# Sort stage of a graph network kernel: keys, places and ranks written four times each in place of full-width copies

## The chip, the cores and the metric

The kernel runs on one core of one Trainium2 chip. The metric is the device time of the whole program in microseconds (us), as the median of several executions; less is better. Engines are named as in the profile: PE is TensorE, PEld its weight loads, DVE VectorE, ACT ScalarE, POOL GpSimd, SP the engine that issues most DMAs.

## The reference

A two-block graph network over N = 6250 nodes with 64 features and E = 200000 edges (`src`, `dst`; the edges come sorted by `dst`).

```python
h = jnp.maximum(_layernorm(x, axis=-1), 0.0)
x = x + segment_sum(h[src], dst, 6250)
h = jnp.maximum(_layernorm(x, axis=-1), 0.0)
# three layers, out = x = h, row = src, col = dst
for l in range(3):
    f1 = relu(x[row] @ nb_W[l] + nb_b[l])
    f2 = relu(x[col] @ self_W[l] + self_b[l])
    a = relu(concatenate([f1, f2], axis=1) @ att1_W[l] + att1_b[l])
    mask = clip(sigmoid(a @ att2_W[l] + att2_b[l]) * (ZETA - GAMMA) + GAMMA, 0.0, 1.0)
    d_inv_sqrt = clip((segment_sum(mask, row) + 1e-06) ** (-0.5), 0.0, 10.0)
    x = segment_sum(mask * d_inv_sqrt[row] * d_inv_sqrt[col] * x[col], row)
    out = out + x
```

Everything after the sort works on blocks of 128 nodes, and gathers and scatters are matrix products with one-hot matrices. For this the edges must first be sorted into bins, one for each pair (block of `src`, block of `dst`).

## The kernel before, in words

`gnn` runs its stages one after another: `constants`, `load_inputs`, `sort_edges`, `first_table`, `build_and_sum` (which builds the one-hot matrices), then per layer `node_products`, `masks_and_messages` and a path for edges that found no place in their bin. Each stage ends in a barrier of all engines. The change lies in `sort_edges` alone.

**The work of the sort.** There are NB = 49 blocks of nodes. For each block c of `dst`, called a row here, each of the 128 partitions holds a window of WIN = 36 consecutive edges (6 columns by 6 groups) that may belong to the block. NBP = 52 is 49 rounded up. A row has these steps:

- POOL `fetch_key` writes `local`, the 36 keys relative to block c (the block of `src`, if the edge belongs to c), and `fetch_places` writes `place_w`, the places of the edge in its two blocks (two ends, 36 each).
- ACT `widen_blocks` writes each of the 36 keys 52 times side by side into `block_wide`. DVE `pick_blocks` compares that with the numbers 0 to 51 (`k.number`): `hot`, a one-hot row of 52 per edge. Then five compares give `twin`, which tells for the columns 1 to 5 apart whether two edges of one partition have one key.
- PE `count_sooner` (L432, L436) counts with 36 products into `sooner_ps` how many edges come sooner. ACT `take_prefix` (L494) copies that to `sooner`. DVE `pick_ranks` multiplies it with `hot` (`picked`, L570) and adds halves (`folded`, L575). PE `add_ranks` (L447, L451) sums `folded` and `twin` into `rank_ps`, 36 ranks.
- ACT copies the ranks to `rank_few` (L505) and writes each rank 128 times into `rank_wide` (L506). DVE `spread_out` (L581) compares them with `k.ranks`: `spread`, a one-hot row of 128 per edge.
- DVE `set_values` writes `hot` times the place for each end into `value`. The first end reads `place_wide`, which ACT `widen_places` (L488) has written 52 times each (L564). The second end reads `place_w` itself, with a step of 0 over the 52 elements (L561).
- PE `scatter` (L461) sums `value` times `spread` over the 36 edges into `bins_ps`; ACT `take_bins` copies the bins to bytes, SP stores them, POOL `note_spills` (four dependent steps, L394 to L397) marks edges whose rank has no place.

**The order.** Each engine has its own order of these steps, written by hand; `each_row` unrolls row 0 and loops over the rest two at a time (buffers b = 0 and 1), and counting semaphores tie the engines. `row(c)` is:

```python
# DVE                        # PE                         # ACT
pick_ranks(c, b)             add_ranks(c, b)              rank_few(c); rank_wide(c)
pick_blocks(c + 1, 1 - b)    count_sooner(c + 1, 1 - b)   take_prefix(c + 1, 1 - b)
spread_out(c - 1, 1 - b)     scatter(c - 1, 1 - b)        widen_blocks(c + 2, b)
set_values(c, b)                                          widen_places(c + 1, 1 - b)
                                                          take_bins(c - 1, 1 - b)
```

POOL's `row(c)` is `fetch_key(c + 2)`, `fetch_places(c + 1)`, `note_spills(c - 1)`. So one row's ranks go round a ring: `folded` on DVE, `add_ranks` and then the next row's `count_sooner` on PE, `take_prefix` on ACT, `picked` and `folded` on DVE again. `block_wide` and `place_wide` have one buffer each; `widen_blocks(c)` waits for `hot` of row c - 1, `widen_places(c)` for the values of row c - 1.

Of the kernel before, what the change touches and what calls it, by code (L numbers as in the profile page):

```python
# [14 lines left out]
P = 128  # L15
# [6 lines left out]
WIN = COLS * GROUPS  # L22
BLOCK_KEY = 64
# [315 lines left out]
def sort_edges(nc, k):  # L339
# [6 lines left out]
    with ExitStack() as st:  # L346
# [6 lines left out]
        local = sb("local", [P, 2, WIN], BF16)  # L353
# [4 lines left out]
        block_wide = sb("block_wide", [P, WIN, NBP], BF16)  # L358
        place_wide = sb("place_wide", [P, WIN, NBP], BF16)
        rank_wide = sb("rank_wide", [P, 2, WIN, P], BF16)  # L360
# [13 lines left out]

        with phase(nc, "passed keyed placed blocks_wide places_wide hot_ready twins_ready values_ready prefixed prefix_ready "
# [5 lines left out]
            def _(pool):  # L381
                def fetch_key(c, b):
                    at = bass.ds(pool.value_load(k.starts[0:1, bass.ds(c, 1)]), WIN)
                    pool.tensor_tensor(local[:, b, :], k.key[:, at], k.bases[:, bass.ds(c, 1)].to_broadcast([P, WIN]),
# [90 lines left out]
            def _(act):  # L475
# [3 lines left out]
                def widen_blocks(c, b):  # L479
                    act.wait_ge(s["keyed"], c + 3)  # L480
                    act.wait_ge(s["hot_ready"], c + 2)
                    nc.scalar.activation(block_wide[:, :, :], local[:, b, :].unsqueeze(2).to_broadcast([P, WIN, NBP]),
                                         ACT.Copy).then_inc(s["blocks_wide"], 1)

                def widen_places(c, b):
                    act.wait_ge(s["placed"], c + 3)
                    act.wait_ge(s["values_ready"], c + 2)
                    nc.scalar.activation(place_wide[:, :, :], place_w[:, b, 0, :].unsqueeze(2).to_broadcast([P, WIN, NBP]),  # L488
# [12 lines left out]
                def row(c, b, nth, first):  # L501
# [4 lines left out]
                    nc.scalar.activation(rank_wide[:, b, :, :], rank_ps[b][:, :].unsqueeze(2).to_broadcast([P, WIN, P]),  # L506
# [32 lines left out]
            def _(dve):  # L539
# [3 lines left out]
                def pick_blocks(c, b):  # L543
# [4 lines left out]
                    nc.vector.tensor_tensor(by_column[:, b, :, :], k.number[:, 0:NBP].unsqueeze(1).to_broadcast([P, WIN, NBP]),  # L548
                                            block_wide[:, :, :], ALU.is_equal).then_inc(s["hot_ready"], 1)
                    dve.wait_ge(s["ranked"], c + 1)  # L550
                    for by in range(1, COLS):
                        z = (COLS - by) * GROUPS
                        last = nc.vector.tensor_tensor(twin[:, b, by - 1, 0:z], local[:, b, by * GROUPS:WIN],
                                                       local[:, b, 0:z], ALU.is_equal)
                    last.then_inc(s["twins_ready"], 1)

                def set_values(c, b):
                    dve.wait_ge(s["hot_ready"], c + 3)
                    dve.wait_ge(s["placed"], c + 3)
# [1259 lines left out]
```

## Time and profile before

| | us |
|---|---|
| median of 3 runs | 4062.88 |
| lowest and highest | 4059.52, 4064.14 |
| time of the profiled execution | 4065.69 |
| its span in the trace | 4063.8 |
| mean granted clock of TensorE | 0.965 |

Busy shares over the whole span are PE 92%, DVE 82%, POOL 60%, ACT 56%. The sort runs from about 37 to 511 us of the span; the rows of `sort_edges` lie in its first eighth. In the profile's slices the granted clock stands at 8 or 7 tenths there and at 9 or more behind it. The granted clock is given as a share of full speed: a mean over a stretch, in which the clock stood at 1.0 (2.4 GHz) for a part and at 0.5 (1.2 GHz) for the rest. In a timeline, each line has the start, the duration, the engine, the line of the code, what is written and read, the count, and in brackets how long the engine sat idle before it and what ended that.

### The profile page before, as it was taken

Reading aid. Unit: us, or ns where it says so; the run is one execution under the profiler, and the core shown is the slowest. Engines: PE = TensorE matmul, PEld = TensorE weight load, DVE = VectorE, ACT = ScalarE, POOL = GpSimd, SP = SyncE. Lnnn points to the kernel's source line nnn. Section 1 sums busy time; section 2 is a strip of 40 time slices with the busy share of each in tenths; the row PEclk is TensorE's granted clock in tenths of the full one; section 3 lists DMA queues with packets and bytes.
Section 4 is the critical chain, followed back from the end, with each engine's and each line's share of the span. In section 5 each row is a group of like instructions: output and inputs, shape, how many; then the busy total and the mean of one; then the engine's idle time right before and its main releaser. Section 6 shows DMA issues by size and latency. Waiting matters only on the chain. (4 is left out here: it accounts for less than half of the span.)

```text
span 4063.8 us, 258198 instructions
## 1 busy us (share of the span) xinstructions
PE 3726.6 (92%) x99855; PEld 3570.8 (88%) x99856; DVE 3323.0 (82%) x5561; ACT 2293.6 (56%) x5432; POOL 2420.1 (60%) x4693
## 2 busy tenths in 40 slices
PE   4888758888879999999998999999998999999998
PEld 4777658888859999899997999999997999989998
DVE  7999968888867888788877888878886788878887
ACT  4988858888841111388881111168884111138887
POOL 2667723333325666577774666667775566657776
PEclk8888879999989999999999999999999999999999
DMA  1000169999937777677754777767773777767775
GB/s 36 15 15 14 16 211 333 342 338 335 336 114 234 241 243 249 194 190 190 190 160 162 243 240 248 248 167 190 190 190 111 238 243 248 243 193 191 190 190 154
DMA packets 586269, 800.05 MB, mean 197 GB/s; under 512 B 126790, under 2 KB 528154, under 8 KB 586170
## 3 DMA queue, kind: packets, MB, share of 16 engines
q1 hardware_dynamic: 550106, 719.89, 56.9%
q0 software_dynamic: 36064, 78.85, 6.6%
q8 instruction: 61, 1.00, 0.1%
q14 instruction: 38, 0.31, 0.0%
HBM read 672.34 MB, written 126.04 MB: 196 GB/s over the span
## 5 line engine op out<-in xcount | busy, mean ns | idle before, releaser
L1359 PE MATMUL pre_ps<-rows_a,hot_ab 128*128 128x64 bf16 x21609 | 1296.1, 193 | 48.1 <-ACT rows_a L1452 23.2
L1359 PE MATMUL pre_ps<-table,hot_ab 128*128 128x64 bf16 x21609 | 1294.9, 193 | 1.7 <-issue 1.7
L1359 PEld LDWEIGHTS pre_ps<-rows_a,hot_ab 128*128 128x128 fp8e4 x21609 | 1127.6, 98 | 78.1 <-issue 54.7
L1593 POOL TENSOR_TENSOR message<-message 128x448 f32<-128x448 f32 x1029 | 948.5, 934 | 322.2 <-DVE message L1661 321.7
L1359 PEld LDWEIGHTS pre_ps<-table,hot_ab 128*128 128x128 fp8e4 x21609 | 1129.1, 98 | 0.6 <-issue 0.6
L1643 DVE SCALAR_TENSOR_TENSOR message<-pre_ps,all_w 128x448 f32<-128x448 f32 x1029 | 642.9, 625 | 280.6 <-PE pre_ps L1359 193.2
L1403 PE MATMUL pre_ps<-table,hot_ab 128*128 128x64 bf16 x21609 | 805.7, 194 | 19.8 <-DVE message L1661 9.1
L1403 PEld LDWEIGHTS pre_ps<-table,hot_ab 128*128 128x128 fp8e4 x21609 | 763.9, 98 | 22.8 <-issue 22.1
L1500 ACT ACTIVATE message<-pre_ps 128x448 bf16<-128x448 f32 x1029 | 674.1, 674 | 165.0 <-DVE pre_ps L1655 139.2
L1655 DVE TENSOR_TENSOR pre_ps<-pre_ps,mask 128x448 f32<-128x448 f32 x735 | 465.0, 633 | 209.5 <-PE pre_ps L1403 187.4
L1626 DVE TENSOR_REDUCE logit<-message 128x7 f32<-128x448 f32 x1029 | 626.8, 609 | 0.0
L1661 DVE TENSOR_TENSOR message<-pre_ps,message 128x448 f32<-128x448 f32 x1029 | 620.9, 615 | 2.2 <-ACT message L1500 0.5
L1448 ACT ACTIVATE gate<-logit,all_b 128x49 f32<-128x49 f32 x147 | 49.9, 339 | 720.1 <-DVE logit L1626 720.1
L897 POOL DMA_DIRECT2D places<-slots_scratch x294 | 213.9, 742 | 398.5 <-DVE hot L1014 319.2
L1489 ACT ACTIVATE pre_ps<-pre_ps,mask 128x64 f32<-128x64 f32 x2058 | 442.7, 309 | 0.2
L1415 PE MATMUL pre_ps<-message,hot_ab 128*128 128x192 bf16 x3675 | 402.6, 248 | 2.8 <-POOL message L1593 2.0
L1014 DVE TENSOR_SCALAR hot<-places,pcol 128x1792 uint8<-128x1792 uint8 x343 | 379.8, 1149 | 10.6 <-DMA places<-slots_scratch 10.6
L1415 PE MATMUL total_ps<-message,hot_ab 128*128 128x192 bf16 x3528 | 382.6, 246 | 0.7 <-issue 0.7
L989 ACT ACTIVATE counts<-cnt_ps 128x896 bf16<-128x896 f32 x343 | 314.1, 916 | 1.5 <-PE cnt_ps L951 1.0
L1415 PEld LDWEIGHTS pre_ps<-message,hot_ab 128*128 128x128 fp8e4 x3675 | 293.4, 97 | 5.4 <-issue 4.7
L1465 ACT ACTIVATE table<-left 128x64 f32 (+1 forms) x147 | 37.8, 257 | 444.1 <-POOLq L1570 444.1
L965 PE MATMUL l_ps<-rows,counts 128*128 128x64 bf16 x7203 | 269.6, 194 | 15.2 <-issue 9.9
(195 smaller groups left out, 5526.0 us busy)
## 6 DMA issues: line engine op xcount, KB each, us to landing
hot_ab<-hot_scratch SPq DMA_DIRECT2D x2058, 224.0 KB, 4.0
hot_scratch<-hot SPq DMA_DIRECT2D x343, 336.0 KB, 5.8
both<-hot_scratch SPq DMA_DIRECT2D x147, 784.0 KB, 5.1
places<-slots_scratch POOLq DMA_DIRECT2D x196, 224.0 KB, 6.3
places<-slots_scratch POOLq DMA_DIRECT2D x98, 336.0 KB, 7.3
slots_scratch<-bins SPq DMA_DIRECT2D x392, 16.0 KB, 1.4
out<-res SPq DMA_DIRECT2D x1, 1536.0 KB
raw<-in_src SPq DMA_DIRECT2D x1, 768.0 KB
```

Source lines behind the costliest of these rows:

```text
L989: nc.scalar.activation(counts[:, n.half, :, :], cnt_ps[n.half][:, 0:G, :], ACT.Copy)\
L1014: dve.tensor_scalar(hot[:, n.slot, 0:2, :], places[:, n.h, :, n.g * G * P:(n.g + 1) * G * P], k.pcol1[:, 0:1], float(HOT), ALU.is_equal, A ...
L1359: last = nc.tensor.matmul(pre_ps[g][:, j, :], hot[:, b, g, end, j * P:(j + 1) * P].bitcast(FP8), table, start=end + part == 0, stop=end == ...
L1403: last = nc.tensor.matmul(bank(g, b)[:, j, :], hot[:, 1 - b, g, 0, j * P:(j + 1) * P].bitcast(FP8), k.table_s[:, g * G + j, part, :], star ...
L1415: last = nc.tensor.matmul(sum_ps[b], hot[:, 1 - b, g, 1, j * P:(j + 1) * P].bitcast(FP8), top[:, g, j, :, :, 1], start=t == 0, stop=t == N ...
L1489: last = nc.scalar.activation(bank(g, b)[:, j, :], bank(g, b)[:, j, :], ACT.Copy, scale=k.mask[:, bass.ds(r * NB + g * G + j, 1)])
L1500: nc.scalar.activation(top[:, g, :, 0, :, 1], bank(g, b), ACT.Copy).then_inc(s["tops_ready"], 1)
L1593: pool.tensor_tensor(message[:, g, :, 2, :], message[:, g, :, 1, :], top[:, g, :, 1, :, 1], ALU.subtract).then_inc(s["third_ready"], 1)
L1626: dve.tensor_reduce(logit[:, b, g * G:(g + 1) * G], weighed[(b + g) % 2], X, ALU.add)\
L1643: dve.scalar_tensor_tensor(weighed[(b + g) % 2], pre_ps[g][:, 0:G, :], 0.0, k.w3[:, :].unsqueeze(1).to_broadcast([P, G, D]), ALU.max, ALU. ...
L1655: dve.tensor_tensor(bank(g, b), bank(g, b), k.mask[:, bass.ds(r * NB + g * G, G)].unsqueeze(2).to_broadcast([P, G, D]), ALU.mult).then_inc ...
L1661: dve.tensor_tensor(message[:, g, :, 1, :], bank(g, b), top[:, g, :, 0, :, 1], ALU.subtract).then_inc(s["rest_ready"], 1)
```

## The change

Where before an engine read 52 or 128 full copies of a value, it now reads four copies of it, again and again:

- ACT writes each key (`block_four`), each place of both ends (`place_four`) and each rank (`rank_four`) four times side by side instead of 52 or 128 times. `block_four` and `place_four` have two buffers, and ACT's waits for them are one row older.
- DVE reads them with a pattern of three dimensions: 36 edges, then 13 (or 32) repeats with a step of 0, then 4 elements with a step of 1. Output and the other input are cut into runs of four in the same way.
- Both ends of `set_values` now read `place_four` in this way; the second one read `place_w` with a step of 0 before. DVE no longer waits for `placed` itself.
- One compare of 180 elements takes the place of the five for `twin`. It reads `local` in five overlapping stretches of 36 from element 6, 12, ... 30 on; `local` has 30 more elements for this, set to zero once by a memset ahead of the rows.

Nothing outside `sort_edges` changes; the stage of messages is the same in both kernels.

```diff
-        local = sb("local", [P, 2, WIN], BF16)
+        TURN = WIN - GROUPS
+        local = sb("local", [P, 2, WIN + TURN], BF16)
...
-        block_wide = sb("block_wide", [P, WIN, NBP], BF16)
-        place_wide = sb("place_wide", [P, WIN, NBP], BF16)
-        rank_wide = sb("rank_wide", [P, 2, WIN, P], BF16)
+        block_four = sb("block_four", [P, 2, WIN, FOUR], BF16)
+        place_four = sb("place_four", [P, 2, 2, WIN, FOUR], BF16)
+        rank_four = sb("rank_four", [P, 2, WIN, FOUR], BF16)
...
+        def fours(t):
+            return t.rearrange("p w (m f) -> p w m f", f=FOUR)
+
+        def along(four, m):
+            return four.unsqueeze(2).to_broadcast([P, WIN, m, FOUR])
+
+        def later_columns(b):
+            row = local[:, b, GROUPS:GROUPS + WIN]
+            return bass.AP(row.tensor, row.offset, [row.ap[0], [GROUPS, COLS - 1], [1, WIN]])
...
                 def widen_blocks(c, b):
                     act.wait_ge(s["keyed"], c + 3)
-                    act.wait_ge(s["hot_ready"], c + 2)
-                    nc.scalar.activation(block_wide[:, :, :], local[:, b, :].unsqueeze(2).to_broadcast([P, WIN, NBP]),
+                    act.wait_ge(s["hot_ready"], c + 1)
+                    nc.scalar.activation(block_four[:, b, :, :], local[:, b, 0:WIN].unsqueeze(2).to_broadcast([P, WIN, FOUR]),
                                          ACT.Copy).then_inc(s["blocks_wide"], 1)
 
                 def widen_places(c, b):
                     act.wait_ge(s["placed"], c + 3)
-                    act.wait_ge(s["values_ready"], c + 2)
-                    nc.scalar.activation(place_wide[:, :, :], place_w[:, b, 0, :].unsqueeze(2).to_broadcast([P, WIN, NBP]),
+                    act.wait_ge(s["values_ready"], c + 1)
+                    nc.scalar.activation(place_four[:, b, :, :, :], place_w[:, b, :, :].unsqueeze(3).to_broadcast([P, 2, WIN, FOUR]),
                                          ACT.Copy).then_inc(s["places_wide"], 1)
...
-                    nc.scalar.activation(rank_wide[:, b, :, :], rank_ps[b][:, :].unsqueeze(2).to_broadcast([P, WIN, P]),
+                    nc.scalar.activation(rank_four[:, b, :, :], rank_ps[b][:, :].unsqueeze(2).to_broadcast([P, WIN, FOUR]),
                                          ACT.Copy).then_inc(s["ranks_wide"], 1)
...
-                    nc.vector.tensor_tensor(by_column[:, b, :, :], k.number[:, 0:NBP].unsqueeze(1).to_broadcast([P, WIN, NBP]),
-                                            block_wide[:, :, :], ALU.is_equal).then_inc(s["hot_ready"], 1)
+                    nc.vector.tensor_tensor(fours(by_column[:, b, :, :]),
+                                            fours(k.number[:, 0:NBP].unsqueeze(1).to_broadcast([P, WIN, NBP])),
+                                            along(block_four[:, b, :, :], NBP // FOUR), ALU.is_equal)\
+                        .then_inc(s["hot_ready"], 1)
                     dve.wait_ge(s["ranked"], c + 1)
-                    for by in range(1, COLS):
-                        z = (COLS - by) * GROUPS
-                        last = nc.vector.tensor_tensor(twin[:, b, by - 1, 0:z], local[:, b, by * GROUPS:WIN],
-                                                       local[:, b, 0:z], ALU.is_equal)
-                    last.then_inc(s["twins_ready"], 1)
+                    nc.vector.tensor_tensor(twin[:, b, :, :], later_columns(b),
+                                            local[:, b, 0:WIN].unsqueeze(1).to_broadcast([P, COLS - 1, WIN]), ALU.is_equal)\
+                        .then_inc(s["twins_ready"], 1)
...
                 def set_values(c, b):
                     dve.wait_ge(s["hot_ready"], c + 3)
-                    dve.wait_ge(s["placed"], c + 3)
                     dve.wait_ge(s["scattered"], c + 1)
-                    nc.vector.tensor_tensor(value[:, b, :, HALF:HALF + NBP], by_column[:, b, :, :],
-                                            place_w[:, b, 1, :].unsqueeze(2).to_broadcast([P, WIN, NBP]), ALU.mult)
                     dve.wait_ge(s["places_wide"], c + 3)
-                    nc.vector.tensor_tensor(value[:, b, :, 0:NBP], by_column[:, b, :, :], place_wide[:, :, :], ALU.mult)\
-                        .then_inc(s["values_ready"], 1)
+                    for end in range(2):
+                        last = nc.vector.tensor_tensor(fours(value[:, b, :, end * HALF:end * HALF + NBP]),
+                                                       fours(by_column[:, b, :, :]),
+                                                       along(place_four[:, b, end, :, :], NBP // FOUR), ALU.mult)
+                    last.then_inc(s["values_ready"], 1)
...
-                    nc.vector.tensor_tensor(spread[:, :, :], k.ranks[:, :].unsqueeze(1).to_broadcast([P, WIN, P]),
-                                            rank_wide[:, b, :, :], ALU.is_equal).then_inc(s["spread"], 1)
+                    nc.vector.tensor_tensor(fours(spread[:, :, :]), fours(k.ranks[:, :].unsqueeze(1).to_broadcast([P, WIN, P])),
+                                            along(rank_four[:, b, :, :], P // FOUR), ALU.is_equal).then_inc(s["spread"], 1)
...
                 nc.vector.memset(value[:, :, :, :], 0.0).then_inc(s["step"], 1)
-                dve.wait_ge(s["step"], 1)
+                nc.vector.memset(local[:, :, WIN:WIN + TURN], 0.0).then_inc(s["step"], 1)
+                dve.wait_ge(s["step"], 2)
```

DVE's instructions of one row in the loop before, from `picked` to the second value:

```order
L570 TENSOR_TENSOR picked_w<-hot_w,sooner_w 128x1872
L575 TENSOR_TENSOR folded_w<-picked_w 128x936
L544 REGISTER_ALU
L548 TENSOR_TENSOR hot_w<-number,block_wide 128x1872
L553 TENSOR_TENSOR twin<-local 128x30
L553 TENSOR_TENSOR twin<-local 128x24
L553 TENSOR_TENSOR twin<-local 128x18
L553 TENSOR_TENSOR twin<-local 128x12
L553 TENSOR_TENSOR twin<-local 128x6
L580 REGISTER_ALU
L581 TENSOR_TENSOR spread<-ranks,rank_wide 128x4608
L561 TENSOR_TENSOR value_w<-hot_w,place_w 128x36x52
```

The same row in the changed kernel:

```order
L582 TENSOR_TENSOR picked_w<-hot_w,sooner_w 128x1872
L587 TENSOR_TENSOR folded_w<-picked_w 128x936
L556 REGISTER_ALU
L560 TENSOR_TENSOR hot_w<-number,block_four 128x1872
L565 TENSOR_TENSOR twin<-local 128x180
L592 REGISTER_ALU
L593 TENSOR_TENSOR spread<-ranks,rank_four 128x4608
L574 TENSOR_TENSOR value_w<-hot_w,place_four 128x36x52 x2
```

The order is the same; five compares have become one, and the instructions write as many elements as before, the compare for `twin` apart (180 instead of 90).

## Rows read from the trace of the kernel before

**Rows 1.** Windows: from:to, length; PE, PEld, DVE, ACT, POOL busy; granted clock; DMA.

```profile
100.00:450.00 350.00, 302.49 (x4025) 271.19 (x4023) 346.58 (x431) 313.46 (x235) 251.68 (x231) 0.88 0.10 15
```

**Rows 2.** Timeline: DVE from one row's folded to the next row's folded.

```profile
313.84 0.65 DVE L575 TENSOR_TENSOR folded_w<-picked_w 128x936 bf16<-128x936 bf16 x1
...
314.40 1.17 DVE L548 TENSOR_TENSOR hot_w<-number,block_wide 128x1872 bf16<-128x1872 bf16 x1
...
315.50 0.48 DVE L553 TENSOR_TENSOR twin<-local 128x30 bf16<-128x30 bf16 x5
...
315.90 2.60 DVE L581 TENSOR_TENSOR spread<-ranks,rank_wide 128x4608 bf16<-128x4608 bf16 x1
...
318.43 2.11 DVE L561 TENSOR_TENSOR value_w<-hot_w,place_w 128x1872 bf16<-128x1872 bf16 x1
...
320.46 1.19 DVE L564 TENSOR_TENSOR value_w<-hot_w,place_wide 128x1872 bf16<-128x1872 bf16 x1
...
321.57 1.12 DVE L570 TENSOR_TENSOR picked_w<-hot_w,sooner_w 128x1872 bf16<-128x1872 bf16 x1
...
322.73 0.65 DVE L575 TENSOR_TENSOR folded_w<-picked_w 128x936 bf16<-128x936 bf16 x1
```

**Rows 3.** Timeline: the ring of one early row, at half clock throughout.

```profile
61.34 0.65 DVE L575 TENSOR_TENSOR folded_w<-picked_w 128x936 bf16<-128x936 bf16 x1
...
62.23 1.86 PE L447 MATMUL rank_ps<-folded_w,identb 128*128 128x36 bf16 x26 [2.76 <-DVE folded_w L575]
...
64.06 1.72 PE L432 MATMUL sooner_ps<-hot_w,later 128*128 128x312 bf16 x6
...
65.58 4.00 PE L436 MATMUL sooner_ps<-hot_w,onesb 128*128 128x260 bf16 x30
...
69.69 0.52 ACT L494 ACTIVATE sooner_w<-sooner_ps,rank 128x312 bf16<-128x312 f32 x1 [1.21 <-PE sooner_ps L436]
...
70.24 1.13 DVE L570 TENSOR_TENSOR picked_w<-hot_w,sooner_w 128x1872 bf16<-128x1872 bf16 x1 [1.30 <-ACT sooner_w L494]
...
71.41 0.65 DVE L575 TENSOR_TENSOR folded_w<-picked_w 128x936 bf16<-128x936 bf16 x1
```

**Rows 4.** Timeline: PE in two later rows, one fast, one slowed.

```profile
316.55 0.95 PE L432 MATMUL sooner_ps<-hot_w,later 128*128 128x312 bf16 x6
...
317.34 2.19 PE L436 MATMUL sooner_ps<-hot_w,onesb 128*128 128x260 bf16 x30
...
323.52 1.86 PE L447 MATMUL rank_ps<-folded_w,identb 128*128 128x36 bf16 x26 [1.97 <-DVE folded_w L575]
...
325.35 1.72 PE L432 MATMUL sooner_ps<-hot_w,later 128*128 128x312 bf16 x6
...
326.86 3.10 PE L436 MATMUL sooner_ps<-hot_w,onesb 128*128 128x260 bf16 x30
```

**Rows 5.** Groups of instructions on PE, 100 to 450 us: count, busy us, mean ns, idle before.

```profile
L436 PE MATMUL sooner_ps<-hot_w,onesb 128*128 128x260 bf16 (+4 forms) x1170 | 107.8, 259 | 0.0
...
L447 PE MATMUL rank_ps<-folded_w,identb 128*128 128x36 bf16 x1022 | 73.2, 243 | 47.5 <-DVE folded_w L575 47.5
L432 PE MATMUL sooner_ps<-hot_w,later 128*128 128x312 bf16 x234 | 52.1, 376 | 0.0
```

**Rows 6.** Groups of instructions on ACT, 100 to 450 us.

```profile
L506 ACT ACTIVATE rank_wide<-rank_ps 128x4608 bf16<-128x4608 f32 x39 | 156.3, 4007 | 0.0
...
L505 ACT ACTIVATE rank_few<-rank_ps 128x36 f32<-128x36 f32 x39 | 7.9, 202 | 31.8 <-PE rank_ps L451 31.8
```

**Rows 7.** Groups of instructions on POOL, 100 to 450 us: the two fetches.

```profile
L389 POOL COPY place_w<-place 128x72 bf16 x38 | 41.0, 1078 | 19.8 <-issue 13.5 <-DVE value_w L564 5.6 <-ACT place_wide L488 0.7
L384 POOL TENSOR_TENSOR local<-key,bases 128x36 bf16 x38 | 38.9, 1025 | 50.0 <-DVE value_w L564 21.8 <-issue 20.3 <-DVE twin L553 6.8
```

**Rows 8.** Timeline: a POOL fetch beside DVE's spread.

```profile
486.19 2.54 DVE L581 TENSOR_TENSOR spread<-ranks,rank_wide 128x4608 bf16<-128x4608 bf16 x1
...
487.06 1.78 POOL L384 TENSOR_TENSOR local<-key,bases 128x36 bf16 x1 [1.13 <-DVE twin L553]
```

More of the change, by code:

```diff
@@ L22 @@
 WIN = COLS * GROUPS
+FOUR = 4
 BLOCK_KEY = 64
@@ L383, in fetch_key @@
                     at = bass.ds(pool.value_load(k.starts[0:1, bass.ds(c, 1)]), WIN)
-                    pool.tensor_tensor(local[:, b, :], k.key[:, at], k.bases[:, bass.ds(c, 1)].to_broadcast([P, WIN]),
+                    pool.tensor_tensor(local[:, b, 0:WIN], k.key[:, at], k.bases[:, bass.ds(c, 1)].to_broadcast([P, WIN]),
                                        ALU.subtract).then_inc(s["keyed"], 1)
@@ L594, in _ @@
                 spread_out(NB - 1, 0)
-                centre_rows(k, s, Chain(dve, s["step"], 1))
+                centre_rows(k, s, Chain(dve, s["step"], 2))
 def nodes(k, t):
```

## The prediction

> **What bounds the sort now.** I read the windows first, because the change touches only the sort. Between 100 and 450 us DVE is busy for 346.6 of 350 us, ACT for 313.5, PE for 302.5 and POOL for 251.7 [rows 1]. The groups of PE give the number of rows in that stretch: 1170 products of L436 at 30 a row are 39 rows [rows 5], so a row takes 350 / 39 = 8.97 us. All 49 rows lie in the sort; nothing outside it is changed.
>
> Next the timeline of one row on DVE [rows 2]. From one `folded` (313.84) to the next (322.73) are 8.89 us without a gap. The starts give what each instruction costs the row: `folded` 0.56, `hot` 1.10, the five compares of `twin` 0.40, `spread` 2.53, the second end's values (L561) 2.03, the first end's (L564) 1.11, `picked` 1.16. L561 and L564 write equally many elements; L561 reads its place with a step of 0 and takes nearly twice as long. So **DVE sets the row**, and what it loses in instructions the row loses, down to the next limit.
>
> That limit is the ring. Its parts show best in an early row in which PE ran at the half level of its clock throughout [rows 3]: `folded` to PE's first product 0.89; L447 to L432 1.83; the count itself, from L432's start to L436's end, 69.58 - 64.06 = 5.52; then 0.11 to ACT's `take_prefix`, 0.55 to `picked`, 1.17 to `folded`. The sum is 10.07. Without the count it is 4.55. The same count takes 319.53 - 316.55 = 2.98 at the full level, and in a row that the half level covers in part 329.96 - 325.35 = 4.61 [rows 4]. The ring is thus 7.53 in a fast row, 9.16 in a slowed one. A slowed row hardly shows today, since 9.16 is only just over 8.97. The mean count is 107.8 / 39 + 52.1 / 39 less the 0.16 by which the two groups overlap [rows 4, 5], which is 3.94. With a fast count at 2.98 and a slowed one at about 4.5, some 0.64 of the rows must be slowed. The mean clock of 0.88 [rows 1] says the same: a quarter of the time at the half level.
>
> **The change, part by part.**
>
> *L561 becomes a second L564.* Both ends now read four copies with a step of 1. From 2.03 to 1.11 is 0.92 us a row, if a run of four keeps the rate of a long run. No row of this trace has so short a run. The nearest rows from both sides are L564 (52 elements in a run, 1.11) and L561 (a run of one, 2.03). I take 1.11: L561 differs from L564 by the step of 0 between neighbours, and the new pattern has a step of 1 between three of four. The cost if that is wrong is the third rival.
>
> The Trainium skill has two rules on this. The Vector Engine (DVE) Microarchitecture Reference, "Measured stream behaviour on trn2", has a port at full rate as long as its elements come in runs of at least two adjacent 4-byte words on an 8-byte boundary, with any hop between; four bf16 are exactly that. Against the change speaks SBUF — State Buffer, "The DMA port swizzle": lines have 16 bytes and each access that crosses to a new line pays; runs of four hop to another line twice as often as a full line would need. By the first rule the sum stands as I make it; by the second it would move towards the third rival. No row here tells them apart.
>
> *Five compares become one.* Now 0.40. One instruction of 180 elements: at the slope between L564 and `spread`, (2.53 - 1.11) / (4608 - 1872) = 0.52 ns for an element, 180 of them lie 0.88 under L564's 1.11, at 0.23; counted from `folded` (0.56 for 936) the same slope gives 0.17. I take 0.20, between 0.17 and, if overlapping reads cost what five instructions did, 0.40. Gain 0.20 (0 to 0.23).
>
> *`hot` and `spread`* write as many elements as before at the same rate: nothing, with the same condition on runs of four.
>
> *ACT's copies.* 36 elements take 0.202 and 4608 take 4.007 [rows 6], 0.83 ns for each. `rank_four` (144) is then 0.29, `block_four` about 0.3, `place_four` (288) 0.41. ACT drops from 313 of 350 us to some 2.1 us a row. That gives nothing by itself: ACT's work lies beside DVE's. It only makes `take_prefix` start 0.1 after the count in each row, where before it could stand behind 4.0 us of `rank_wide`; I have reckoned the ring with 0.11. If that cover went the other way, ACT has 5 us a row to spare.
>
> *The memset* of 60 elements comes once, at most 0.2 us, behind the large one that is there. *Waits:* those that go were long fulfilled; POOL still waits for `values_ready` before it fetches places, and ACT's older waits only let it run earlier.
>
> **The sum.** DVE needs 8.89 - 0.92 - 0.20 = 7.77 in the row shown; there `hot` and L564 ran at 1.17 and 1.19, where `picked` takes 1.12 for as many elements [rows 2], so about 7.7. The ring at full clock, 7.53, is just under that. At the half level it now sticks out: a slowed row takes about 4.55 + 4.5 - 0.1 (`folded` to PE is 323.52 - 322.73 = 0.79 in the later row [rows 2, 4]) = 8.95. So the gain hangs on how many rows stay slowed:
>
> - none: 7.7, a gain of 1.27 a row;
> - as many as now (0.64): 0.36 x 7.7 + 0.64 x 8.95 = 8.50, a gain of 0.47;
> - my choice, 0.42 of the rows: 0.58 x 7.7 + 0.42 x 8.95 = 8.2, a gain of 0.77.
>
> The reason for my choice: slow stretches follow stretches in which PE waits and then runs only the small products of L447. That wait is 47.5 / 39 = 1.22 us a row now [rows 5]. A fast row now can wait 1.97 [rows 4]; with 1.2 us less to a row it waits about 0.8, while a slowed row waits no less than today. The mean falls by some four tenths, and I let the share of slowed rows fall by a third.
>
> The gain counts in 46 of the 48 row-to-row steps; the first two, like the row of [rows 3], are set by the ring at half clock and stay. 46 x 0.77 = 35 us. Against the profiled execution's 4065.7 that is 4030.7; the median shown is 2.8 us below that execution, which gives **4028**.
>
> **The rivals.**
>
> 1. *The clock recovers.* PE waits so little that the slow stretches vanish. For: the wait falls, and each slow row shortens the wait before the next. Against: the small products stay and are still 1.8 us of a row. Gain 46 x 1.27 = 58 us: 4004.
> 2. *The clock stays as it is,* in share of rows: 46 x 0.47 = 22: 4041. POOL can lead to nearly the same place. Its steps wait for DVE's instructions: a fetch of 36 elements that started 0.87 after `spread` ended 0.11 after its end, 1.78 us long [rows 8]. Of 350 us it was held by a named semaphore for only 5.6 + 0.7 + 21.8 + 6.8 = 34.9 [rows 7], so it needs (350 - 34.9) / 39 = 8.08 us a row, more than DVE's new 7.7. Against that: its six steps mostly end with one DVE instruction each, and DVE still has seven to a row. If POOL sets a row of 8.6, the gain is 46 x 0.37 = 17: 4046. The Trainium skill, SBUF — State Buffer, "Who interferes with whom", says that a DVE instruction with two SBUF inputs keeps out a GpSimd one that reads SBUF; by that rule, the trace agrees.
> 3. *Slower: runs of four run at L561's rate.* Place: `hot`, `spread` and both values. Price: 0.92 for each of the three of 1872 elements and 0.92 x 4608 / 1872 = 2.26 for `spread`, 5.0 us; a row of 12.7, a loss of 3.8 in 46 rows: 4236. It decides from the point at which a quarter of it is lost: 1.27 / 5.0. For: no such pattern in the trace, and the repeat of 13 is a new dimension. Against: above.
> 4. *Half of it:* hops cost a little, say 0.2 to 0.3 of that loss. DVE's row is then 8.7 to 9.2 and the time 4053 to 4075.
>
> **How the numbers follow.** The forecast has a chance of 0.50, rival 1 of 0.17, rival 2 of 0.20, rival 3 of 0.07, rival 4 of 0.06. About 0.2%, some 8 us, is what a measurement of this kernel can tell from no change. The forecast and rivals 1 and 2 lie beyond that on the fast side, 0.87; rival 4 gives 0.03 to the same and 0.02 to slower, the rest to faster; rival 3 is slower. So faster 0.88, same 0.03, slower 0.09. The range takes in rival 1 with a little over it, since DVE's row could come at 7.6 with the shortest steps (46 x 1.37 = 63), and rival 2 with POOL: 3997 to 4046.
>
> **What would show it.** Right: DVE's two value instructions alike at about 1.15 us, one compare for `twin` near 0.25, `spread` still 2.55; ACT's copies at 0.3 to 0.45; DVE no longer without gaps, with idle time before `picked`, released by ACT's `sooner_w`, in just those rows in which the count takes over 4 us; a mean clock between 100 and 400 us above 0.88. The rest of the program unchanged. Wrong: `hot` or `spread` longer than before (rivals 3 and 4); rows of 7.7 throughout at a clock near 1 (rival 1); ACT or DVE waiting for POOL's `local` or `place_w` (POOL in rival 2).

## The result, and the profile after

| | before | changed kernel |
|---|---|---|
| median | 4062.19 us | 4024.85 us (4022.69 to 4027.73, 4 runs) |
| profiled execution | 4065.69 | 4025.11 |
| its span | 4063.8 | 4023.2 |
| ratio to before | | 0.9909, 95% interval 0.9892 to 0.9926 |

Forecast were 4028 us and a range of 3997 to 4046. The change is faster by 37 us.

The windows of the changed kernel, 100 to 400 us of the span; columns as in [rows 1]:

```profile
100.00:400.00 300.00, 271.93 (x3712) 247.77 (x3709) 277.28 (x254) 61.96 (x216) 212.93 (x215) 0.91 0.11 16
```

DVE was busy for 99% of a stretch and is now for 92%; ACT fell from 90% to 21%; the granted clock went from 0.88 to 0.91. DVE is no longer the only thing that sets a row. Its groups of instructions in the same stretch (count, busy us, mean ns, idle before it and what ended that):

```profile
L593 DVE TENSOR_TENSOR spread<-ranks,rank_four 128x4608 bf16<-128x4608 bf16 x36 | 91.7, 2547 | 0.0
L574 DVE TENSOR_TENSOR value_w<-hot_w,place_four 128x1872 bf16<-128x1872 bf16 x74 | 82.5, 1154 | 0.0
L560 DVE TENSOR_TENSOR hot_w<-number,block_four 128x1872 bf16<-128x1872 bf16 x36 | 41.8, 1162 | 0.0
L582 DVE TENSOR_TENSOR picked_w<-hot_w,sooner_w 128x1872 bf16<-128x1872 bf16 x36 | 41.5, 1152 | 21.5 <-ACT sooner_w L506 21.5
...
L565 DVE TENSOR_TENSOR twin<-local 128x180 bf16<-128x180 bf16 x36 | 10.1, 282 | 0.0
```

Both value instructions take 1.15 us, where L561 took 2.11 [rows 2]. `hot` and `spread` are as fast as with full-width copies (1.17 and 2.60 in [rows 2]). DVE now waits 21.5 us, all of it ahead of `picked`, for `sooner_w`. The waits say how often:

```profile
DVE picked_w L582 <- ACT sooner_w L506: 21.5, 15, 1.5
```

15 times in 36 rows, up to 1.5 us. The timeline shows one such row in full, and a fast one ahead of it:

```profile
303.54 0.65 DVE L587 TENSOR_TENSOR folded_w<-picked_w 128x936 bf16<-128x936 bf16 x1
...
311.22 0.65 DVE L587 TENSOR_TENSOR folded_w<-picked_w 128x936 bf16<-128x936 bf16 x1
...
312.15 1.86 PE L459 MATMUL rank_ps<-folded_w,identb 128*128 128x36 bf16 x26 [0.99 <-DVE folded_w L587]
...
313.98 1.08 PE L444 MATMUL sooner_ps<-hot_w,later 128*128 128x312 bf16 x6
...
314.85 3.76 PE L448 MATMUL sooner_ps<-hot_w,onesb 128*128 128x260 bf16 x30
...
318.72 0.52 ACT L506 ACTIVATE sooner_w<-sooner_ps,rank 128x312 bf16<-128x312 f32 x1 [4.05 <-PE sooner_ps L448]
...
319.28 1.13 DVE L582 TENSOR_TENSOR picked_w<-hot_w,sooner_w 128x1872 bf16<-128x1872 bf16 x1 [1.49 <-ACT sooner_w L506]
...
320.44 0.65 DVE L587 TENSOR_TENSOR folded_w<-picked_w 128x936 bf16<-128x936 bf16 x1
```

From 303.54 to 311.22 are 7.68 us: a row at DVE's pace. From 311.22 to 320.44 are 9.22: `folded` to PE 0.93, L459 to L444 1.83, the count 4.63 instead of 2.98, 0.11, 0.56, 1.16. Over the whole sort the 46 steps behind the first two are of just these two kinds: 26 of 7.54 to 7.74 us, 20 of 9.09 to 9.22, mostly by turns. In all of the 20 the count takes 4.62 to 4.64 us and `picked` waits for it; in all of the 26 it takes 2.98 or 2.99 and `picked` waits for nothing.

**Where the time went.** `folded` came first at 51.47 and last at 484.12 us before, at 51.35 and 453.62 now; that is 30.4 us less over 48 steps. The first product behind the sort's barrier started at 511.33 and now starts at 479.67, 31.7 us earlier, since the last `spread` and its scatter also gained. The span is 40.6 us shorter. The other 8.9 lie behind the sort, in code that the change does not touch; the section on the forecast comes back to this.

### The profile page after: what moved, and what is told of

It reads as the page before. It is cut to its first block and busy times, and to the rows that moved or that the text cites. A ratio compares the mean times of both kernels' runs of the same rounds, so it can differ in the third digit from the quotient of the medians.

```text
span 4023.2 us, 257999 instructions
## 1 busy us (share of the span) xinstructions
PE 3711.7 (92%) x99855; PEld 3565.5 (89%) x99856; DVE 3262.2 (81%) x5362; ACT 1976.7 (49%) x5432; POOL 2380.6 (59%) x4693
## 5 line engine op out<-in xcount | busy, mean ns | idle before, releaser
L1027 DVE TENSOR_SCALAR hot<-places,pcol 128x1792 uint8<-128x1792 uint8 x343 | 379.6, 1148 | 8.7 <-DMA places<-slots_scratch 8.7
L1428 PEld LDWEIGHTS total_ps<-message,hot_ab 128*128 128x128 fp8e4 x3528 | 278.0, 96 | 0.1
```

The source lines that it names most:

```text
L1027: dve.tensor_scalar(hot[:, n.slot, 0:2, :], places[:, n.h, :, n.g * G * P:(n.g + 1) * G * P], k.pcol1[:, 0:1], float(HOT), ALU.is_equal, A ...
L1428: last = nc.tensor.matmul(sum_ps[b], hot[:, 1 - b, g, 1, j * P:(j + 1) * P].bitcast(FP8), top[:, g, j, :, :, 1], start=t == 0, stop=t == N ...
```

## The experiments

Three questions stood open. Which parts of the change were needed? Are the rows of 9.1 us really the clock's? Has POOL a part in it? All kernels below build on the changed kernel unless it is said otherwise. To read them I use, beside the time, what a trace tells exactly: the mean of the 46 row steps, the granted clock between 100 and 400 us, and the start of the first product behind the sort (its end).

| kernel | mean row | shortest, longest | clock | sort's end | ratio to before |
|---|---|---|---|---|---|
| before | 8.97 | 8.85, 9.29 | 0.88 | 511.3 | 1 |
| changed | 8.32 | 7.54, 9.22 | 0.91 | 479.7 | 0.9909 (0.9892 to 0.9926) |
| x1, second end with step 0 | 8.87 | 8.59, 9.22 | 0.89 | 505.0 | 0.9979 (0.9969 to 0.9988) |
| x2, ranks 128 times | 8.88 | 8.59, 9.23 | 0.88 | 507.4 | 0.9980 (0.9971 to 0.9990) |
| x3, two products added | 7.67 | 7.54, 7.73 | 1.00 | 450.1 | 0.9848 (0.9832 to 0.9865) |
| x4, no marks | 8.18 | 7.53, 9.29 | 0.91 | 473.5 | |
| y1, changed again | 8.32 | 7.54, 9.23 | 0.91 | 479.0 | 0.9914 (0.9900 to 0.9927) |
| y2, x3 again | 7.67 | 7.60, 7.73 | 1.00 | 448.5 | 0.9843 (0.9829 to 0.9856) |
| y3, before, two products added | 8.91 | 8.85, 9.19 | 0.92 | 505.6 | 0.9997 (0.9988 to 1.0007) |
| y4, y2 with runs of two | 7.67 | 7.61, 7.73 | 1.00 | 448.4 | 0.9849 (0.9831 to 0.9867) |
| z1, y2 with five compares | 8.55 | 7.88, 9.24 | 0.90 | 489.5 | 0.9955 (0.9935 to 0.9974) |
| z2, y2 with ranks 128 times | 8.78 | 8.59, 9.23 | 0.92 | 501.5 | 0.9971 (0.9960 to 0.9983) |
| g1, z1 with four products | 7.94 | 7.88, 7.99 | 1.00 | 461.4 | 0.9884 (0.9866 to 0.9901) |
| g2, y2 with a square on ACT | 7.67 | 7.54, 7.74 | 1.00 | 449.3 | 0.9859 (0.9843 to 0.9876) |

### x1: the second end reads its place with a step of 0 again

```diff
+                    dve.wait_ge(s["placed"], c + 3)
...
-                    for end in range(2):
-                        last = nc.vector.tensor_tensor(fours(value[:, b, :, end * HALF:end * HALF + NBP]),
...
+                    nc.vector.tensor_tensor(value[:, b, :, HALF:HALF + NBP], by_column[:, b, :, :],
+                                            place_w[:, b, 1, :].unsqueeze(2).to_broadcast([P, WIN, NBP]), ALU.mult)
+                    nc.vector.tensor_tensor(fours(value[:, b, :, 0:NBP]), fours(by_column[:, b, :, :]),
+                                            along(place_four[:, b, 0, :, :], NBP // FOUR), ALU.mult)\
+                        .then_inc(s["values_ready"], 1)
```

> The changed kernel with one part undone: the second end of the values reads place_w with a step of 0 again. Theory (DVE sets the fast rows, the ring with the half-level count sets the others): the second value instruction is back at 2.1 us, a fast row is 7.67 + 0.9 = 8.6 us, a slowed one stays near 9.15, PE waits longer and more rows are slowed; the sort is 20 to 28 us longer than in the changed kernel and the time 4045 to 4055. Rival (ACT's relief is what brought the gain, DVE's instructions lie beside it): at most 5 us more than the changed kernel, 4025 to 4030.

4056.64 us, 32 above the changed kernel by the medians, and 28 by the two ratios, each to the kernel before as it ran beside it. DVE's groups:

```profile
L574 DVE TENSOR_TENSOR value_w<-hot_w,place_w 128x1872 bf16<-128x1872 bf16 x34 | 72.9, 2145 | 0.0
L576 DVE TENSOR_TENSOR value_w<-hot_w,place_four 128x1872 bf16<-128x1872 bf16 x34 | 39.6, 1166 | 0.0
```

The one with the step of 0 is back at 2.15 us, and the shortest rows at 8.6, as the theory had it. The sort is 25 us longer than in the changed kernel, inside the 20 to 28 that were expected; the time is 1 to 2 us over its range. The rival falls.

### x2: ACT writes each rank 128 times again

```diff
-        rank_four = sb("rank_four", [P, 2, WIN, FOUR], BF16)
+        rank_wide = sb("rank_wide", [P, 2, WIN, P], BF16)
...
-                    nc.scalar.activation(rank_four[:, b, :, :], rank_ps[b][:, :].unsqueeze(2).to_broadcast([P, WIN, FOUR]),
+                    nc.scalar.activation(rank_wide[:, b, :, :], rank_ps[b][:, :].unsqueeze(2).to_broadcast([P, WIN, P]),
...
-                    nc.vector.tensor_tensor(fours(spread[:, :, :]), fours(k.ranks[:, :].unsqueeze(1).to_broadcast([P, WIN, P])),
-                                            along(rank_four[:, b, :, :], P // FOUR), ALU.is_equal).then_inc(s["spread"], 1)
+                    nc.vector.tensor_tensor(spread[:, :, :], k.ranks[:, :].unsqueeze(1).to_broadcast([P, WIN, P]),
+                                            rank_wide[:, b, :, :], ALU.is_equal).then_inc(s["spread"], 1)
```

> The changed kernel with one part undone: ACT writes each rank 128 times again (4.0 us) and spread reads that. DVE's instructions are as in the changed kernel. Theory (ACT's work is hidden beside DVE's, as the prediction had it): 4025 to 4030. Rival (ACT writes the ranks between add_ranks and take_prefix, so its 4.0 us stand in the ring, which becomes 0.8 + 2.0 + 4.1 + 0.6 + 1.17 = 8.6 us even at full clock): picked waits for sooner_w in nearly every row, rows of 8.6 to 9.1, 4045 to 4058.

4056.42 us: the theory, which was the prediction's own, falls, and the rival stands. The timeline from one `folded` to `sooner_w`:

```profile
302.22 0.65 DVE L587 TENSOR_TENSOR folded_w<-picked_w 128x936 bf16<-128x936 bf16 x1
...
303.01 1.85 PE L459 MATMUL rank_ps<-folded_w,identb 128*128 128x36 bf16 x26 [1.82 <-DVE folded_w L587]
...
305.01 0.20 ACT L517 ACTIVATE rank_few<-rank_ps 128x36 f32<-128x36 f32 x1 [3.28 <-PE rank_ps L463]
305.11 4.00 ACT L518 ACTIVATE rank_wide<-rank_ps 128x4608 bf16<-128x4608 f32 x1
```
```profile
DVE picked_w L582 <- ACT sooner_w L506: 40.2, 34, 1.5
```

DVE has no more work than in the changed kernel, but waits before every `picked` of the stretch, 34 times in 34 rows. `rank_wide` starts 2.9 us behind `folded` and ends 6.9 behind it, and only then can ACT turn to `take_prefix`. With 0.55 us for that and 1.17 for `picked` it makes a row of at least 8.6, even with a fast count; the slowed counts still add to it, up to 9.23. Of ACT's shortened copies only this one was undone by itself.

### x3 and y2: two more products on PE in each row

```diff
+        warm_ps = ps("warm_ps", [P, 4, P])
...
                     if not first:
                         scatter(c - 1, 1 - b)
+                    for _ in range(2):
+                        nc.tensor.matmul(warm_ps[:, :, :], k.identb[:, :],
+                                         k.onesb[:, :].unsqueeze(1).to_broadcast([P, 4, P]), start=True, stop=True)
```

> The changed kernel with two added products of 512 columns on PE at the end of each row, ahead of its wait for folded; they read constants and write a PSUM tensor that nobody reads. Theory (the rows of 9.1 us come from counts at the half level, which follow PE's wait and its small products): the clock stays at 1.0 through the rows behind the first few, all rows take 7.7 us, picked no longer waits for sooner_w, 20 rows save 1.5 us each: time 3992 to 4000. Rival (every other row is long for another reason, POOL or the stores of the bins): rows of 9.1 remain, 4023 to 4030.

> The changed kernel with the two added products on PE, again, beside the changed kernel on the same chip. From the traces the sort is 29.6 us shorter than in the changed kernel; the time should be 25 to 32 us below y1.

4004.41 us for x3 and 3997.04 for y2; beside y2, on the same chip, the changed kernel (y1) had 4027.95. So two products without a use save 31 us by the medians of y1 and y2, 29 by their ratios, and 25 by x3's ratio beside the changed kernel's first one. x3's time is 4 us over its range, y2's difference inside it. The windows of x3, and its timeline between two rows:

```profile
100.00:400.00 300.00, 283.93 (x4116) 254.21 (x4113) 298.65 (x275) 68.16 (x237) 222.62 (x233) 1.00 0.11 17
```
```profile
306.73 2.17 PE L474 MATMUL bins_ps<-spread,value_w 128*128 128x128 bf16 x36
...
308.74 0.59 PE L484 MATMUL warm_ps<-onesb,identb 128*128 128x512 bf16 x2
...
309.85 1.86 PE L460 MATMUL rank_ps<-folded_w,identb 128*128 128x36 bf16 x26 [0.51 <-DVE folded_w L591]
```

The clock stands at 1.00, DVE is busy for 298.65 of 300 us again, and no row behind the first ones takes over 7.73. The two products fill 0.6 us of the wait between the scatter and the next row's products. With the slowed counts all the 9.1 us rows are gone, so nothing else in the changed kernel makes a row long behind the first two.

### x4: no marking steps on POOL

```diff
-                    step(pool.tensor_scalar(off[:, :], rank_few[:, b, :], -(RANK0 + 0.5 * (k.CAP - 1)), None, ALU.add))
-                    step(pool.tensor_tensor(off[:, :], off[:, :], off[:, :], ALU.mult))
-                    step(pool.tensor_scalar(kept[:, :], off[:, :], 0.25 * (k.CAP - 1) ** 2, None, ALU.is_le))
-                    step(pool.tensor_tensor(k.spill[:, at], k.spill[:, at], kept[:, :], ALU.subtract))
```

> The changed kernel without POOL's four steps that mark edges whose rank has no place; the marks are left out. Theory (POOL follows DVE and sets nothing): rows of 7.7 and 9.1 as before, time 4022 to 4028. Rival (POOL's steps, held up by DVE's instructions, hold back the row): the rows of 9.1 shrink or vanish, 3995 to 4015.

Only the sort can be read here: without the marks every edge goes down the slow path for edges without a place, and the whole took 202733 us, which I had not thought of when I gave the times. The long rows are still there (18 of 46), so POOL does not make them. But the short ones are 7.54 instead of 7.67, and the sort ends 6.2 us sooner: some 3.6 of that are 28 short rows at 0.13, the rest is that two rows fewer are long. DVE's groups show the difference, small in each instruction:

```profile
L556 DVE TENSOR_TENSOR hot_w<-number,block_four 128x1872 bf16<-128x1872 bf16 x37 | 42.1, 1138 | 0.0
L578 DVE TENSOR_TENSOR picked_w<-hot_w,sooner_w 128x1872 bf16<-128x1872 bf16 x37 | 41.7, 1127 | 22.6 <-ACT sooner_w L502 22.6
```

`hot` took 1162 ns and `picked` 1152 in the changed kernel. POOL paces nothing, but its steps cost DVE 0.13 us a row. Which of DVE's instructions pays differs with the moment at which they meet: with rows of 7.67 throughout (y2) `hot` took 1141 and `picked` 1137, but the values 1169 instead of 1148 and `twin` 299 instead of 244. The Trainium skill, SBUF — State Buffer, "Who interferes with whom", has a DVE instruction with two SBUF inputs and a GpSimd one that reads SBUF keep each other out; by that rule, the trace agrees, in both directions now.

### y1: the changed kernel again

> The changed kernel, unaltered, on the chip on which the next ones run. Theory: the sort is 31.7 us shorter than before in the trace, and the median's other 5 to 9 us are variation of the later stages between executions: ratio to before 0.991 to 0.993. Rival (the sort's change also shortens what follows): ratio 0.990 again and a later part, from the barrier behind the sort to the end, below 3545 us in the trace.

4027.95 us, ratio 0.9914. The sort's end (479.0) and its rows are the first trace's to a hundredth. The ratio fits the theory; the part behind the sort, 4025.1 - 479.0 = 3546.1, is just over the rival's mark of 3545, between the changed kernel's first trace (3543.5) and before's (3552.5).

### y3: the kernel before with the two products

The same edit as x3's, made to the kernel before.

> The kernel before with the same two added products. Theory (before, DVE with 8.87 us a row set the pace and the slowed counts only just showed): all rows 8.85 to 8.9, 0.1 us a row, 4 to 6 us less than before. Rival (the clock itself cost before what it costs in the changed kernel): 25 to 30 us less.

```profile
100.00:400.00 300.00, 263.95 (x3537) 229.48 (x3535) 298.06 (x369) 270.64 (x202) 234.54 (x201) 0.92 0.10 15
```

4062.35 us against 4063.18: no difference that can be measured, although the sort ended 5.7 us sooner in the trace, as the theory said; behind the sort this trace was the longest of all. The rival falls. The clock is not fully held here (0.92), and PE waits longer for `folded` in these rows (34.5 us in 33 rows, 16.1 in 39 in x3). That it hardly shows is because DVE with 8.87 covers most of a slowed count: 21 of the 46 counts are still slowed, and `picked` waits behind only 6 of them.

### y4: runs of two instead of four

This kernel is y2's with one number changed.

```diff
-FOUR = 4
+FOUR = 2
```

> The changed kernel with the two added products on PE (so that DVE sets every row) and two copies in place of four, so that DVE reads runs of two. Theory (DVE's rate asks only for a step of 1 between the two elements of a pair): rows of 7.67, hot and values at 1.13 to 1.17, time as y2. Rival (a run must have at least two words of 4 bytes, the rule of the Trainium skill, Vector Engine (DVE) Microarchitecture Reference, on measured stream behaviour): hot and the values take 1.7 to 2.0 us, spread 4 or more, a row 11 to 12.5 us, time 4150 to 4230.

```profile
L597 DVE TENSOR_TENSOR spread<-ranks,rank_four 128x4608 bf16<-128x4608 bf16 x39 | 99.3, 2546 | 0.0
L578 DVE TENSOR_TENSOR value_w<-hot_w,place_four 128x1872 bf16<-128x1872 bf16 x78 | 88.2, 1169 | 0.0
L564 DVE TENSOR_TENSOR hot_w<-number,block_four 128x1872 bf16<-128x1872 bf16 x40 | 45.6, 1140 | 0.0
```

4001.94 us, rows of 7.67. (The names in the rows still say four.) A run of two bf16 keeps the full rate, as one of four does and one of 52. Only a step of 0 between neighbours (2145 ns in x1) loses it. The rule of the Trainium skill in the Vector Engine (DVE) Microarchitecture Reference, "Measured stream behaviour on trn2", that a run must have two words, was measured there on streams of 32-bit elements; it does not hold for this pattern of bf16, in which the second input reads one word over and over. The measurement decides.

### z1 and g1: five compares again, and four added products

```diff
-                    nc.vector.tensor_tensor(twin[:, b, :, :], later_columns(b),
...
+                    for by in range(1, COLS):
+                        z = (COLS - by) * GROUPS
+                        last = nc.vector.tensor_tensor(twin[:, b, by - 1, 0:z], local[:, b, by * GROUPS:WIN],
+                                                       local[:, b, 0:z], ALU.is_equal)
+                    last.then_inc(s["twins_ready"], 1)
```

> The changed kernel with the two added products on PE and the five compares for twin back. DVE sets every row, so the row shows the price of the five compares: 7.67 + 0.2 = 7.87 us, 9 us more than with one compare. Rival (the short gaps between the five compares let POOL through and save DVE as much): 7.67 to 7.72.

4042.12 us: neither. The fast rows are 7.88 to 7.90, so the five compares do cost 0.22 us a row. But now every other row takes 9.2, and the mean is 8.55, so 0.22 us on DVE cost 0.88. The windows show why the two added products did not help any more:

```profile
100.00:400.00 300.00, 283.55 (x3690) 246.36 (x3689) 277.14 (x386) 60.30 (x210) 188.92 (x210) 0.90 0.10 15
```

The clock is at 0.90 again. With DVE's part of the row 0.22 us longer and PE's work the same, PE's clock falls back to the half level. g1 tests this, with the same five compares and `range(4)` in place of `range(2)`:

> z1 (five compares for twin, two added products on PE) with four added products instead of two. z1 had rows of 7.89 and 9.2 by turns, mean 8.55. Theory (the 9.2 are slowed counts again, since 0.22 us more on DVE lengthened PE's wait just enough for the clock to fall): with PE's wait filled all rows take 7.89, the clock is 1.0, the sort is 30 us shorter than in z1 and 10 us longer than in y2; time 4005 to 4012. Rival (the five compares hold up something else, POOL's fetches or ACT, in every other row): rows of 9.2 remain, 4038 to 4045.

```profile
100.00:400.00 300.00, 290.25 (x4038) 252.39 (x4036) 298.71 (x417) 65.02 (x228) 181.51 (x228) 1.00 0.11 17
```

The clock is at 1.00, the long rows are gone, and rows take 7.91 and 7.97 by turns, 7.94 in the mean. The sort is 28 us shorter than z1's and 13 longer than y2's. The time, 4014.67, is 3 us above what was expected. Some 0.05 us a row over the 7.89 are not explained; PE waited only 7.9 us in 38 rows, so four products may be a little too many.

### z2: ranks 128 times, with the two products

> The changed kernel with the two added products on PE and the ranks written 128 times again. Theory (ACT's 4.0 us stand in the ring between add_ranks and take_prefix, whatever the clock): every row 8.6 us, picked waits for sooner_w in all of them, clock 1.0, sort 40 us longer than with four copies. Rival (what x2 lost was lost through PE's clock, because PE waited longer): rows of 7.7 to 7.9.

4050.58 us. No row is under 8.59, which the clock cannot be the cause of: rows with a fast count are here as in x2. `picked` waited for `sooner_w` in each of the 34 rows of the stretch, 36.5 us in all. So ACT's 4.0 us in the ring are a limit of their own. The expectation was wrong in one thing: the clock was not held (0.92), PE waited longer for `folded` than in x3 (31.1 us in 34 rows), and some rows are still 9.0 to 9.2. The sort is so 53 us longer than y2's, where 40 were expected.

### g2: two of POOL's steps less

ACT squares the rank less the middle while it copies it out of PSUM, and POOL compares that at once; the bound is raised from 4032.25 to 4064.25, between two values that can occur.

```diff
-                    step(pool.tensor_scalar(off[:, :], rank_few[:, b, :], -(RANK0 + 0.5 * (k.CAP - 1)), None, ALU.add))
-                    step(pool.tensor_tensor(off[:, :], off[:, :], off[:, :], ALU.mult))
-                    step(pool.tensor_scalar(kept[:, :], off[:, :], 0.25 * (k.CAP - 1) ** 2, None, ALU.is_le))
+                    step(pool.tensor_scalar(kept[:, :], rank_few[:, b, :], 0.25 * (k.CAP ** 2 - 2 * k.CAP + 1) + 0.25 * k.CAP, None, ALU.is_le))
...
-                    nc.scalar.activation(rank_few[:, b, :], rank_ps[b][:, :], ACT.Copy)
+                    nc.scalar.activation(rank_few[:, b, :], rank_ps[b][:, :], ACT.Square, bias=k.middle[:, 0:1])
```

> The changed kernel with the two added products on PE, and with two of POOL's four marking steps moved: ACT squares the rank less the middle while it copies it out of PSUM (in place of a plain copy), POOL compares and subtracts only. Theory (DVE sets every row, and POOL's steps cost DVE's instructions about 0.03 us each time they meet; without any marking steps the row was 7.54 in place of 7.67): rows of 7.60, the sort 3 us shorter than in y2, the time 3 us less, hardly to be told from y2's. Rival (the price comes from the two fetches alone): rows of 7.67.

POOL is busy for 98.68 of 300 us, where it was 222.96 in y2, and the mean row is still 7.67 (7.61 and 7.73 by turns). The theory falls: the 0.13 us that POOL costs DVE do not shrink with the number of steps. The rival's row is met, but g2 does not prove that the two fetches cause it, since x4 kept both fetches and had 7.54.

## Why the prediction was right

**DVE's row.** Forecast 7.7 us, measured 7.67 (7.54 to 7.74). L561's change was put at 0.92: 2.03 between starts became 1.1, and x1 shows the reverse. The runs of four, the largest risk of the forecast (rival 3, 4236 us), cost nothing at all; y4 shows that not even runs of two do. One argument for that rival was no argument: by the note on 16-byte lines that the prediction takes from the Trainium skill (SBUF — State Buffer, "The DMA port swizzle"), short runs were to hop to another line twice as often. But the new pattern reads one group of 8 bytes 13 or 32 times before it moves on, and the output and the other input lie as before. It changes lines less often than the full copies did, and no run here tests that note. The one compare was put at a gain of 0.20; z1's fast rows say 0.22.

**The ring and the clock.** That slowed counts would stick out, in idle time before `picked`, released by `sooner_w`, and in no other rows, is what the trace shows. x3 shows the cause: with the clock held the long rows vanish. The share of slowed rows was forecast as 0.42 and came to 20 of 46, 0.43; before it was 28 of 46, 0.61, where the prediction had 0.64. PE's wait for `folded` did fall as reckoned, from 1.22 us a row to 28.1 / 36 = 0.78. That the share would fall by a third with it was a choice and followed from no number, so that part was luck. The price of a slowed row was put too low: forecast 8.95, measured 9.09 to 9.22. The step that was mis-sized is "4.55 + 4.5 - 0.1". The count of 4.5 was a mean over counts that the half level covered in part (4.03 to 4.64 before); now each slowed one takes 4.62 to 4.64. And the way from `folded` to PE is 0.79 in only 7 of the 20 rows and 0.89 to 0.94 in the others. The mean row was then 8.32 instead of 8.2, and the gain 46 x 0.65 = 30 us instead of 35.

**The sum.** 31.7 us in the sort were measured, 35 forecast, and yet the time fell by 37 and 40.6 in the profiled executions. From the copy of the counts behind the sort to the last sum, code that is alike in all kernels, before took 3528.6 us, the changed kernel 3519.7 and 3522.3, and the thirteen traces with an unharmed end 3519.2 to 3533.9. The 8.9 us between the first two are spread over the layers, in no stretch between two of their gates more than 3.4 us. So the forecast's median was met to 3 us with some help from there: 5 us too much in the sort and 6 us of the median that nobody forecast nearly cancel, and that is luck. The four traces without added products and with the changed sort (3519 to 3523) lie below all others. The ratios point the same way: these four kernels gained 2 to 5 us more than their sort did in the trace, and the eight with added products between 2 us more and 5 less. Whether the changed sort, or the added products, act on what follows was not tested.

**The step that failed.** "That gives nothing by itself: ACT's work lies beside DVE's." x2 shows the contrary. The four copies of the ranks are worth as much as the whole change: without them it gains 0.2%, as it does without the second end (x1). I had read ACT's busy share as cover, and had not put its order into the ring: `rank_wide` stands between `add_ranks` and `take_prefix` on one engine. The rows shown ahead of the prediction had it: 0.89 and 1.83 until the ranks are summed [rows 3], 0.2 and 4.0 for ACT's two copies [rows 6], 0.55 and 1.17 behind them [rows 3] make 8.6, right under DVE's 8.89. The kernel before had two limits 0.3 us apart, and the change lifted both. The number came out right because the ring was reckoned from an early row whose long count hid the copy, and with the copy gone that sum was the right one.

**The rivals.** Rival 1 (the clock recovers, 4004) did not come by itself; made by hand in x3 and y2 it gave 3997 to 4004. Rival 2: the share of slowed rows fell by a third and no more. POOL sets no row (x4), and the 8.08 us that the prediction reckoned it to need are not a limit: rows take 7.67 in x3 with all of POOL's steps. What it took for POOL's work is in part time in which a step is held up by a DVE instruction: a step that took 1.78 us in [rows 8] takes 0.28 us elsewhere (L396 at 311.69 in the changed kernel). Rivals 3 and 4 fall with the durations of the groups.

**The better version.** The changed kernel with the two added products is the fastest of these, 0.9843 and 0.9848 of before, against 0.9909 and 0.9914. It is also touchy: z1 shows that 0.22 us more on DVE takes some 40 us of the sort away again, unless the products are made four, and then 28 of them come back.

## What to carry to other kernels

Draw the ring of dependent steps with every instruction that stands between two of them on the same engine, even where that engine is idle in the sum; here a copy that nobody on the ring waits for was 4.0 of 8.6 us. When one limit is lifted, look how near the next ones are: here two parts lifted two limits that lay side by side, and with either part taken out the whole change gave 0.2% instead of 0.9%. And where PE waits for another engine in each round, look at the granted clock of the rounds: a filler of 0.6 us in the wait gave another 25 to 31 us here, not much less than the change itself. In the kernel before, where other limits covered the slowed counts, the same filler gave nothing that could be measured.

## What the runs showed of the hardware

- A two-input instruction of DVE on bf16 keeps its full rate on inputs that read the same two or four elements again and again (1140 to 1169 ns for 1872 elements); with one element read again and again it takes 2145.
- One compare over five overlapping stretches of 36 elements takes 0.24 us where POOL hardly meets it (244 ns mean in x4, without POOL's marking steps; 282 in the changed kernel).
- TensorE's clock fell to its half level in rows in which PE waited no longer than 0.6 to 1.0 us and was busy otherwise, part of it with products of 36 columns. Two products of 512 columns in that wait held it at 1.00 through 46 rows (x3, y2); with DVE's part of the row 0.22 us longer they did not (z1, 0.90), and four did (g1, 1.00).
